# Level 1 of a two-layer convolution kernel: chunks of 8, 8, 8, 6 and 4 slot rows, next-image x chunks behind the relu rows, second-layer weights on GpSimd

## What is computed

```
for i in range(LEVELS):                       # levels 0 to 3; this document is about level 1
    y = x if i == 0 else mean over blocks of 2**i x 2**i
    y = relu(conv3x3(y, ds_w3[i], dilation d)) # level 1: d = 5, a 64 x 64 image
    feats.append(conv1x1(y, ds_w1[i]))
att(f): ker = kg_w2 @ gelu(kg_w1 @ mean(f[:16]))          # 3x3 taps for each of 16 channels
        out = concat(conv13x13(f[:16]) + depthwise(f[:16], ker), f[16:])
layer 1: y3 = conv3x3(x, w3); y5 = conv5x5(x, w5)
         out = wr[0] * y5 + sum over the 9 shifts of wr[1 + shift] * shifted y3
```

## Time and profile before

| | us |
|---|---|
| median of 3 runs | 2785.94 (2785.59 to 2786.02) |
| the profiled execution, device time | 2779.98 |
| the profiled execution, span from first to last instruction | 2778.2 |
| level-1 block | about 543 |
| one of its images 1 to 6 | 58.00 |
| PE busy over the span | 2493.0 (90%) |
| DVE, ACT, POOL busy over the span | 2124.8, 1104.4, 888.8 |

### The profile page before, as it was taken

One profiled execution on the slowest core, in us unless ns is written; L12 is line 12 of the kernel. 1 busy time (PEld: TensorE's weight loads), 2 busy tenths in 40 slices (PEclk: granted clock), 3 DMA queues, 4 the chain that ended last, 5 costly groups with the idle time before them and its releaser, 6 DMA issues. The chain is left out here.

```text
span 2778.2 us, 37571 instructions
## 1 busy us (share of the span) xinstructions
PE 2493.0 (90%) x11638; PEld 2008.3 (72%) x11638; DVE 2124.8 (76%) x2823; ACT 1104.4 (40%) x1773; POOL 888.8 (32%) x824
## 2 busy tenths in 40 slices
PE   3889999599996999999995988898839999999998
PEld 3677777488885888888884767676627777777776
DVE  5655555645446888888887798999878989999898
ACT  1322223111104999999985222222113333333331
POOL 6765554122203444444444754444000000000000
PEclk9899999788877999999997998999959999999999
DMA  7443333100006877777783144443442333333332
GB/s 137 102 109 91 79 91 71 37 6 13 14 8 133 231 214 209 221 222 218 220 219 115 35 153 153 159 158 146 175 177 64 96 111 115 95 96 103 116 103 61
DMA packets 345087, 338.82 MB, mean 122 GB/s; under 512 B 57648, under 2 KB 308400, under 8 KB 331696
## 3 DMA queue, kind: packets, MB, share of 16 engines
q1 hardware_dynamic: 337056, 335.53, 41.6%
q10 hardware_dynamic: 7952, 2.30, 0.5%
HBM read 211.60 MB, written 122.62 MB: 120 GB/s over the span
## 5 line engine op out<-in xcount | busy, mean ns | idle before, releaser
L169 PE MATMUL ps_all<-vh,u_h 128*128 128x512 f32 x960 | 385.0, 401 | 28.4 <-DVE vl L2944 27.9
L171 PE MATMUL ps_all<-vh,u_l 128*128 128x512 f32 x960 | 383.5, 399 | 0.0
L170 PE MATMUL ps_all<-vl,u_h 128*128 128x512 f32 x960 | 383.0, 399 | 0.0
L2853 ACT ACTIVATE vh<-rt,gn 128x528 fp32r<-128x528 f32 x192 | 131.0, 728 | 445.5 <-DVE rt L2921 319.6
L169 PE MATMUL ps_all<-vh,t_h 128*128 128x512 f32 x576 | 231.5, 402 | 24.2 <-DVE vl L1983 24.2
L169 PEld LDWEIGHTS ps_all<-vh,u_h 128*128 128x128 f32 x960 | 181.0, 189 | 82.0 <-issue 35.5
L1822 POOL TENSOR_TENSOR zr<-zr,z 128x256 f32<-128x256 f32 x128 | 124.0, 988 | 337.9 <-DMA xr<-in_x 337.9
L170 PE MATMUL ps_all<-vl,t_h 128*128 128x512 f32 x576 | 230.3, 400 | 0.0
L171 PE MATMUL ps_all<-vh,t_l 128*128 128x512 f32 x576 | 229.4, 398 | 0.0
L171 PEld LDWEIGHTS ps_all<-vh,u_l 128*128 128x128 f32 x960 | 181.1, 189 | 46.3
L170 PEld LDWEIGHTS ps_all<-vl,u_h 128*128 128x128 f32 x960 | 181.3, 189 | 45.5
(11 more groups left out here) (410 smaller groups left out, 6642.6 us busy)
## 6 DMA issues: line engine op xcount, KB each, us to landing
xr<-in_x SPq DMA_DIRECT2D x128, 256.0 KB, 3.6
x_layer<-xr SPq DMA_DIRECT2D x64, 512.0 KB, 2.7
xq<-x_layer SPq DMA_DIRECT2D x32, 1024.0 KB, 4.8
x_layer<-xq SPq DMA_DIRECT2D x32, 1024.0 KB, 3.8
out<-ot SPq DMA_DIRECT2D x64, 512.0 KB, 5.2
xw<-in_x SPq DMA_DIRECT2D x112, 288.0 KB, 4.4
xw<-x_layer SPq DMA_DIRECT2D x16, 1152.0 KB, 8.6
xw<-x_layer SPq DMA_DIRECT2D x16, 1088.0 KB, 7.6
```

The source lines that it names most:

```text
L169: pe.matmul(o, wh, xh, start=first, stop=False, skip_group_check=True)
L170: pe.matmul(o, wh, xl, start=False, stop=False, skip_group_check=True)
L171: return pe.matmul(o, wl, xh, start=False, stop=last, skip_group_check=True)
L2853: act.activation(vh[:, v % 2, n, :, :].rearrange("p a b -> p (a b)"), rt[:, n, :, :].rearrange("p a b -> p (a b)"), ACT.Identity, scale=gn ...
```

## The change

Four tables of numbers change: the convolution chunks are 8, 8, 8, 6 and 4 slot rows in place of 7, 7, 7, 7 and 6, with the rows of the normalization (`pieces`) and of the relu (`rows_at`) to match. `prep_at` leaves only chunks 2, 3 and 4 between the relu rows. POOL does chunks 5, 6 and 7 behind the last `rl`; DVE does chunk 5 behind the pooled value, chunks 6 and 7 and the aggregate (`stats_begin`) behind `fl`. The statistics matmuls move in the filter from tiles 1 and 10 to tiles 6 and 12. The second-layer weights of the last image move from DVE to POOL, where the clearing stands ahead of the first `rl` and all 35 steps behind the last; ACT's `z_out` of the last image moves ahead of its wait for them. The attention keeps its place behind the first chunk.

```diff
-            chunks = [(0, 7), (7, 14), (14, 21), (21, 28), (28, UROWS)]
+            chunks = [(0, 8), (8, 16), (16, 24), (24, 30), (30, UROWS)]
-            pieces = [(2, 12), (12, 19), (19, 26), (26, 33), (33, 37)]
-            rows_at = [(0, 5), (5, 12), (12, 19), (19, 26), (26, N1)]
+            pieces = [(2, 13), (13, 21), (21, 29), (29, 35), (35, 37)]
+            rows_at = [(0, 6), (6, 14), (14, 22), (22, 28), (28, N1)]
...
-                return [(2,), (3,), (4, 5), (6,), (7,)][k]
+                return [(2,), (3,), (4,), (), ()][k]
...
@@ gpsimd
+                    def conv5_clear():
...
+                        pool.memset(s31, 0.0).then_inc(l1_z, 1)
+                        pool.memset(c5, 0.0).then_inc(l1_z, 1)
...
                     def body(i, nxt, nxt2, first=False):
+                        last = not nxt
                         pool.wait_ge(n_l, NCH * (i + 1))
                         alone(pool)
+                        if last:
+                            conv5_clear()
...
+                        if last:
+                            conv5_first()
+                            for sh in range(3):
+                                for sw in range(3):
+                                    conv5_shift(sh, sw)
...
+                        if nxt:
+                            for c in range(5, NX):
+                                prep_chunk(i + 1, c)
@@ scalar
                         if last:
+                            z_out(i)
                             steps.at(act, 0, NSTEP)
...
-                            z_out(i)
@@ vector
-                        if last:
-                            conv5_clear()
...
-                            if last and k == 0:
-                                conv5_first()
-                                conv5_shift(0, 0)
...
                         if nxt:
-                            stats_begin(i + 1)
+                            prep_chunk(i + 1, 5)
...
                             ins.then_inc(f_l, 1)
+                        if nxt:
+                            prep_chunk(i + 1, 6)
+                            prep_chunk(i + 1, 7)
+                            stats_begin(i + 1)
                         chain_taps_dve(dve, i, 1, chain, ker_s, ps_ch)
...
@@ tensor
-                            between[1] = lambda: group_mean_pe(pe, stats, i + 1, avg)
-                            between[10] = lambda: group_var_pe(pe, stats, i + 1, avg)
+                            between[6] = lambda: group_mean_pe(pe, stats, i + 1, avg)
+                            between[12] = lambda: group_var_pe(pe, stats, i + 1, avg)
```

More of the change, by code:

```diff
@@ L632, in norm_low, with step @@
                                                nview(nh, s0, s1_).bitcast(F32), ALU.subtract).then_inc(n_l, 1)
+                    def step(ins):
+                        steps.done(ins)
+                        steps.wait(pool)
+                    def conv5_clear():
+                        steps.start(0)
+                        pool.wait_ge(l1_e, 16 * 8)
+                        pool.wait_ge(n_l, NCH * B)
+                        pool.wait_ge(p2_done, B)
+                        pool.wait_ge(n_f, NCH * B)
+                        pool.wait_ge(bn_done, 4 + 2 * NX * B)
+                        alone(pool)
+                        pool.memset(s31, 0.0).then_inc(l1_z, 1)
+                        pool.memset(c5, 0.0).then_inc(l1_z, 1)
+                        step(pool.memset(row_w[:, :, :], 0.0))
+                        step(pool.memset(cls, 0.0))
@@ new lines, in conv5_first, with conv5_shift @@
+                    def conv5_first():
+                        pool.wait_ge(l1_ld, 16 * 4)
+                        pool.wait_ge(l1_lw, 16)
+                        step(pool.tensor_tensor(c5.rearrange("p a b c -> p (a b) c"),
+                                               c5.rearrange("p a b c -> p (a b) c"),
+                                               wrb[:, 0, :].unsqueeze(1).to_broadcast([P, 30, C]), ALU.mult))
+                    def conv5_shift(sh, sw):
+                        step(pool.tensor_tensor(tmp.rearrange("p a b c -> p (a b) c"),
+                                               s31.rearrange("p a b c -> p (a b) c"),
+                                               wrb[:, shift_tap(sh, sw), :].unsqueeze(1).to_broadcast([P, 12, C]), ALU.mult))
+                        d = c5[:, 2 - sw:6 - sw, 2 - sh:5 - sh, :]
+                        step(pool.tensor_tensor(d, d, tmp, ALU.add))
+                        for side, h0, kx in ((0, 2, 2), (1, 0, 0)):
+                            if sh == h0:
+                                d = cls[:, side, 2 - sw:6 - sw, :]
+                                step(pool.tensor_tensor(d, d, tmp[:, :, kx, :], ALU.add))
+                        for r, w0, a in ((0, 2, 3), (1, 0, 0)):
+                            hp = par(r)
+                            if sw == w0:
+                                d = row_w[hp, 2 - sh:5 - sh, :]
+                                step(pool.tensor_tensor(d, d, tmp[hp, a, :, :], ALU.add))
+                                for side, h0, kx in ((0, 2, 2), (1, 0, 0)):
+                                    if sh == h0:
+                                        step(pool.tensor_scalar(cor_w[hp, side, :], tmp[hp, a, kx, :], -1.0,
+                                                               None, ALU.mult))
@@ L643, in body @@
                                     prep_chunk(i + 1, c)
+                        if last:
[3 more added lines that the diff above has]
+                                    conv5_shift(sh, sw)
+                            assert steps.n == NSTEP, steps.n
+                        if nxt:
+                            for c in range(5, NX):
+                                prep_chunk(i + 1, c)
                         if first:
@@ L846, in norm @@
                             a, b = max(s0, d), min(s1_, d + N1)
+                            if a >= b:
+                                continue
                             ins = dve.tensor_scalar(pln[hp, a - 2:b - 2, :], pl1[hp, a - d:b - d, :],
@@ L904, in output_weights @@
                                                      ALU.mult, ALU.subtract).then_inc(a_g, 1)
[L906 to L948, removed]
@@ L1028, in body @@
                                 output_weights(r)
[L1029 to L1033, removed]
                         dve.wait_ge(l_h, i + 1)
```

3 lines of the change are left out of this document (removed).

## The result

The changed kernel takes 2751.32 us (median of 4 runs, 2747.30 to 2758.28), beside 2785.77 for the kernel before on the same chip (2777.60 to 2786.02). The ratio is 0.9886, with a 95% interval of 0.9859 to 0.9913: faster by 24 to 39 us. 24.4 were forecast. The profiled execution is the slowest of the four, 2758.28 with a span of 2756.5.

What follows compares the result with a forecast made beforehand. PE bounds the kernel: its own work plus one 4.60 us hole an image, which also costs clock. 35.4 us gained in images 1 to 6 less 11 in the last: 2785.94 - 24.4 = 2761.5 us, range 2753 to 2778.

Steps and rivals of the forecast that it cites:

- The hole: PE's wait ahead of features half 1 in each steady image: from 4.60 to 1.35 us, bounds 0.7 to 2.0.
- the sum: Images 1 to 6 gain 6 x 5.9 = 35.4 us, image 0 gives 0, the last loses 11: 24.4 gained.
- The clock behind the hole: PE's features half 1 and identity, behind the hole, run at full granted clock; this decides 2.5 us an image.
- rival 1: The clock falls all the same behind the hole: 3.4 us gained an image, 2776.5 us in all; chance 0.18.
- the 2.09 us of one-column matmuls: The attention's taps in each image pass at clock 1.00, as does the filter behind; used to expect full clock.
- Statistics at tiles 6 and 12: Mean's and variance's matmuls, moved within the filter, cause no wait; 1.7 us of slack at worst.
- the 0 of the sum: Image 0, whose filter waits for POOL's low filter parts: no change, between -1.5 and +1 us.
- The weights on POOL: Last image's second-layer weights, 35 steps on POOL, done at T + 77.6: 11 us lost, between 5.5 and 17.5.
- 15.98 later: Time from the `conv_weights` DMA's issue (539.54) to the next levels' first matmul (555.52) in the kernel before.
- Rival 2: Weights steps on POOL run at the collided price, x 1.59: 39 us lost in the last image, slower; chance 0.07.
- the reading by which all six kernel-tile steps add themselves: Exclusive lock between DVE and POOL: some 5 us of DVE steps join POOL's weights chain, time 3 us later, 2764.5.

Runs made afterwards that it cites:

- e3: Kernel before with only the new order (x chunks behind relu rows, statistics at tiles 6 and 12), old chunk tables, weights on DVE: 2751.8 us.
- e9: Changed kernel with last image's weights shared between POOL and DVE, copies and store first, taps split five and four in images 1 to 7: 2739.7 us.

## Why the prediction came out

The forecast of 2761.5 lies 10.2 us above the measured median, 2751.32, which is itself 1.7 us below the lower end of the forecast's range, 2753; by the ratio, 0.9886 of the 2785.94 on which the forecast was made, the time is 2754.2, just inside it. The main step of the prediction is shown: the hole was made by the next image's work ahead of the last `rl` and `rsum`, and e3, which changes that order alone, closes it. Term by term:

- **The hole**, forecast at 1.35 us with bounds 0.7 and 2.0, is 0.95 from the end of half 0 to the start of half 1, of which PE idles 0.75. Half 0 ends at t = 21.0 instead of 20.8 (195.91, with the image's start at 174.90), and half 1 starts at 21.96 instead of 22.15. The fourth `rl` ends at 195.85, t = 20.95, where 21.1 was forecast: the chain went as the sum had it.
- **The clock behind the hole** holds in all images, as the sum had it (rival 1 put it at 0.50). The row it was taken from was thin, since behind that idle stretch of 1.48 us only 0.97 us of matmuls are shown at 1.00; e3, with 1.20 us of waiting and its features at 1.00, bears it out better. But the clock falls two steps later, behind the taps, in three images of six, 1.1 us each: 3.4 us that the sum lacked. The step that failed is "the 2.09 us of one-column matmuls in each image pass at 1.00 with 1.00 in the filter behind": true in the kernel before, but there a stretch at 0.50 and 0.74 stood ahead of the taps, and no row showed the taps behind one at 1.00. Where the clock stays, an image takes 52.3; 52.1 was forecast. So 30.9 were gained instead of 35.4.
- **Statistics at tiles 6 and 12** have no wait, as forecast: neither of the two matmuls (208.61 and 213.68 in image 2) shows idle time ahead. Image 0 ends at 121.44 us instead of 121.66, near the 0 of the sum.
- **The weights on POOL**: the loss was there, and mis-sized, 4.1 us instead of 11. Two terms of the sum make the difference. The chain ends at T + 73.3 instead of T + 77.6: steps of 768 elements took 1.80 to 1.86 but for one, near their price, but 0.08 us lie between dependent steps instead of 0.18, 35 x 0.10 = 3.5 us. The 0.18 was read between the three sums of a chunk, between which the program also increments another semaphore (`alone`), which it does not between steps of the weights; that this makes the difference was not tried. And the "15.98 later" was no fixed distance: it is SP's issue, then 12.93; the issue shrank from 3.05 to 0.34 since the store of `z` is long done, 2.7 us. Rival 2 (collided prices) did not come: four of 35 steps are stretched, the longest from 1.83 to 2.43, by 2.3 us in all. That is near the 2 that the sum had for DVE beside POOL, and not the 5 of the reading by which all six kernel-tile steps add themselves.
- **The sum**: 30.9 less 4.1 is 26.8 beside a forecast of 24.4; that they lie so close is luck in part, since two misses of 4.5 and 6.9 us stand against each other. The trace has 27.0, with the 0.2 of image 0. The runs' medians differ by 34, but they hold the levels behind as well, whose time varies from run to run as shown above; how much of the 7 us between comes from there can't be told run by run.

## What to carry over

Where an engine that feeds the critical one does work for the next round, put that work behind the last thing the critical engine waits for; the size of the last chunk matters only after that. A step moved off a busy engine is not free where the idle engine is twice as slow and the step's end closes the stage: share it by what each engine can finish by the same time. Price the way from a last step to the next stage by its parts, the issue of a DMA among them, and not as one fixed distance.

## What was not expected of the hardware

- One and the same DMA issue of SP took 0.34, 1.80 or 3.0 to 3.2 us, by how close behind another store's issue it came.
- Two executions of one program alternate their clock falls in opposite phase (images 1, 3, 5 and images 2, 4, 6), each fall worth 1.1 us.
- Four breaks of a stream of 512-column matmuls, by two taps each (the last by one), cost 1.1 us more than all nine taps in one place; one break by four taps cost 0.3 (e9).
- Dependent POOL steps that wait on their own engine's semaphore follow each other after 0.08 us (464.70 + 1.80 to 466.58), where the dependent sums of a chunk, with an increment of another semaphore between them, stand 0.18 apart.
